# A gated attention and mixture-of-experts block: the running maximum spread by transfers and masked on GpSimd instead of by matmuls

## The chip, the cores and the metric

The kernel runs on one core of a Trainium2 chip. The metric is device time in microseconds (us). Before the change it is 1078.76 us, the median of three runs (1076.42 to 1082.22).

## The reference

For 16 batch elements of 256 tokens and 512 features, x goes through a gated mLSTM attention (8 heads of 64) against ctx, and then through a mixture of 16 experts (2 per token) with a shared expert. Cut to what matters here:

```
ig, fg = [q,k,v] @ gate weights + bias          # q = layernorm(x), k = v = ctx; per head and token
cs     = cumsum(log_sigmoid(fg))                # along the tokens
log_D  = cs[s] - cs[t] + ig[t], for t <= s, else -inf
D      = exp(log_D - max_t(log_D))
C      = (q k^T / 8) * D
h      = C v / (max(|sum C|, exp(-max)) + 1e-6)
x      = x + tanh(g0) * layernorm(h) * ln_scale
x      = x + tanh(g1) * (top-2 of 16 experts(layernorm(x)) + shared(layernorm(x)))
```

With key[t] = ig[t] - cs[t], the exponent is key[t] - M[s], where M[s] is the running maximum of key up to s. The kernel holds scores with t on the partitions and s along the row. So it needs M, one row per head, on all 128 partitions, and a very large value where s < t, so that the exponential gives zero there.

## The kernel before

One program has three stages: a loop over the 16 batch elements (attention, router, shared expert), the routed experts over 79 tiles of 128 rows, and a last stage that does the shared expert for four late batches (9, 11, 13, 15) and combines. Each engine has its own list of instructions, written out by hand in a function `step`, and waits on semaphores (`event`).

A step t of the loop holds work of several batches at once: A = t attends, F = t+1 is prepared (`turn_ctx`, `turn_x`, gates, `rows`, `columns`), N = t+2 gets its input statistics, G = t-1 is normalized after the attention, routed and put through the first half of its shared expert, H = t-2 has the second half of its shared expert, is ranked, and its rows are scattered to its experts in DRAM. For the late batches the shared expert is left out of the loop, so that steps 10, 12 and 14 lack `shared(G, 0)` and `shared(G, 1)`, and steps 11, 13 and 15 lack the shared work of H.

M is made on VectorE by a scan over 8 rows (`rows`, L1464). It is then split into three bf16 parts: ACT rounds the first (`max_hi`, L769), VectorE makes the other two (`rows_end`, L1472, L1475, L1477). PE spreads each head's M over the partitions (`spread`): for each head one product with a selecting matrix for 256 columns and one for 128 (L1091), and after each a product that adds the mask (L1093), into one of two PSUM banks, `MB`. ACT reads that bank in `head` (L782, L784) and writes the decay exp(key - M); VectorE multiplies it with the scores (`head`, L1492); PE multiplies with the values (`pv`, L1103 to L1106). PE's spreads stand in four blocks of two heads in a step: before `shared(H, 2)`, before `pv(A, 0)`, before `scores_pair(A, 2)`, and before `gates_sum(F)`. A pair of heads has one pair of score banks, `QK`, so `scores_pair(A, q)` waits until VectorE is done with pair q-1.

On GpSimd a step has the two small powers for G, the four indirect scatters of H, the copy of F's values (`values`, L567) and the power for N, in that order. SP's list holds the loads of ctx and x (`load_next`), 4 MB of zeros and a pad of 256 KB for the experts' rows (L457, L459), and the store of the shared weights in two parts, `kept_w` (L462). `load_next(b)` waits for the copy of batch b-2's values.

After the loop VectorE makes the tables of tiles, then the low part of expert 0's weights (L1841), then adds the last batch's shared sums and weighs. GpSimd issues the last eight scatters and then splits expert 1's weights. ACT issues the loads of the first four tiles of rows (16 transfers, L412) and then copies the tiles that VectorE has turned (L919); SP loads the later tiles. PE begins with `gate_up` (L1289).

## Time and profile before

| what | us |
|---|---|
| median of three runs | 1078.76 (1076.42 to 1082.22) |
| the profiled execution | 1078.9 |
| its span in the profile | 1077.3 |
| PE busy | 960.1 (89%) |
| VectorE (DVE) busy | 813.8 (76%) |
| ScalarE (ACT) busy | 424.7 (39%) |
| GpSimd (POOL) busy | 423.3 (39%) |
| attention loop, start to the last step's end | about 0 to 580 |
| routed experts | about 616 to 970 |
| late shared expert and combination | about 970 to 1077 |

Busy time is the time in which an engine has an instruction under way; matmuls overlap each other and their ends are modelled. The span is what the profile covers of the execution. An engine's share is a mean over stages with different limits, so that the rows are read by stage.

### The profile page before, as it was taken

Reading aid. Unit: us, or ns where it says so; the run is one execution under the profiler, and the core shown is the slowest. Engines: PE = TensorE matmul, PEld = TensorE weight load, DVE = VectorE, ACT = ScalarE, POOL = GpSimd, SP = SyncE. Lnnn points to the kernel's source line nnn. Section 1 sums busy time; section 2 is a strip of 40 time slices with the busy share of each in tenths; the row PEclk is TensorE's granted clock in tenths of the full one; section 3 lists DMA queues with packets and bytes.
Section 4 is the critical chain, followed back from the end, with each engine's and each line's share of the span. In section 5 each row is a group of like instructions: output and inputs, shape, how many; then the busy total and the mean of one; then the engine's idle time right before and its main releaser. Section 6 shows DMA issues by size and latency. Waiting matters only on the chain.

```text
span 1077.3 us, 21069 instructions
## 1 busy us (share of the span) xinstructions
PE 960.1 (89%) x6143; PEld 804.9 (75%) x6143; DVE 813.8 (76%) x1995; ACT 424.7 (39%) x957; POOL 423.3 (39%) x315
## 2 busy tenths in 40 slices
PE   3589999999999998989987199999999999999981
PEld 2479888988888886967777178888888888777761
DVE  2887889888988899888867666666666666655885
ACT  2654445444544455444522034444444444342110
POOL 5010220222022202222123907767767777104775
PEclk9989999999999998989969599999999999999996
DMA  8670211221122112111014455577667675924888
GB/s 256 223 287 2 80 40 40 79 79 40 40 79 79 39 42 79 60 59 41 11 42 159 159 169 179 179 211 212 180 183 228 177 206 155 335 77 149 261 284 263
DMA packets 92778, 147.26 MB, mean 137 GB/s; under 512 B 10720, under 2 KB 51168, under 8 KB 91776
## 3 DMA queue, kind: packets, MB, share of 16 engines
q0 software_dynamic: 17872, 65.02, 18.7%
q1 hardware_dynamic: 60592, 58.74, 17.3%
q10 hardware_dynamic: 14208, 22.16, 5.9%
q8 instruction: 57, 0.93, 0.4%
q14 instruction: 49, 0.40, 0.1%
HBM read 89.26 MB, written 56.62 MB: 135 GB/s over the span
## 4 chain that ended last, share of the span: by engine, by line
PE 69%; DVE 12%; issue 7%; DMA 4%; POOL 4%; ACT 1%; ACTq 1%; SPq 0%; DVEq 0%; POOLq 0%
PE bank L1289 19%; PE bank L1159 13%; PE bank L1308 9%; PE bank L1172 5%; PE bank L1082 4%; PE bank L1014 4%; POOL w_ring L698 3%; PE bank L1103 2%; PE bank L1106 2%; PE bank L1104 2%; PE bank L1356 2%; DMA x2n<-routed_x 2%; PE bank L1132 2%; PE bank L1299 2%; DMA base_out<-in_x_dram 2%
## 5 line engine op out<-in xcount | busy, mean ns | idle before, releaser
L1289 PE MATMUL bank<-w_ring,x2nT 128*128 x948 | 254.0, 406 | 19.9 <-DVE x2nT L1871 19.6
L1289 PEld LDWEIGHTS bank<-w_ring,x2nT 128*128 128x128 f32 x948 | 173.2, 190 | 57.7 <-issue 22.4
L1159 PE MATMUL bank<-x2nT,w_ring 128*128 128x256 f32 x1152 | 149.8, 286 | 0.0
L579 POOL DMA_INDIRECT routed_x<-x2n,slot_u x64 | 68.9, 1077 | 205.6 <-DVE slot_u L1632 190.6
L1159 PEld LDWEIGHTS bank<-x2nT,w_ring 128*128 128x128 f32 x1152 | 142.4, 190 | 0.3
L1308 PE MATMUL bank<-w_ring,sh_actT 128*128 x474 | 121.1, 391 | 3.5 <-DVE sh_actT L1860 3.5
L1860 DVE TENSOR_TENSOR sh_actT<-bank,sh_actT 128x256 fp32r<-128x256 f32 x79 | 33.5, 425 | 108.8 <-ACT sh_actT L929 108.8
L661 POOL TENSOR_TENSOR w_ring<-area,one 128x3072 fp32r<-128x3072 f32 x14 | 74.2, 5303 | 87.3 <-PE bank L1308 87.3
L1308 PEld LDWEIGHTS bank<-w_ring,sh_actT 128*128 128x128 f32 x474 | 88.8, 188 | 24.0 <-issue 4.6
L698 POOL DMA_INDIRECT w_ring<-routed_y,y_slot x64 | 67.8, 1060 | 77.6 <-DMA routed_y<-cs_in 52.6
L664 POOL TENSOR_TENSOR w_ring<-area,w_ring 128x3072 fp32r<-128x3072 f32 x14 | 95.8, 6845 | 2.5 <-POOL w_ring L661 2.5
L1866 DVE STREAM_TRANSPOSE bank<-x2n 128x512 f32<-128x512 f32 x79 | 86.6, 1096 | 3.6 <-DMA x2n<-routed_x 3.5
L934 ACT COPY cs_in<-bank 128x512 f32<-128x512 f32 x79 | 46.4, 588 | 84.2 <-PE bank L1308 77.3
L1172 PE MATMUL bank<-w_ring,sh_actT 128*128 128x512 f32 x288 | 72.5, 401 | 5.5 <-issue 5.5
L1492 DVE SCALAR_TENSOR_TENSOR area<-bank,area 128x384 f32<-128x384 f32 x128 | 65.8, 551 | 11.5 <-PE bank L1082 6.2
L586 POOL TENSOR_TENSOR x_rstd_all<-x_var,minus_half 128x2 f32<-128x2 f32 x16 | 12.8, 799 | 152.6 <-DVE x_var L1556 152.6
L923 ACT ACTIVATE ctxT<-bank 128x256 f32<-128x256 f32 x79 | 30.3, 384 | 102.7 <-PE bank L1289 102.7
L1082 PE MATMUL bank<-area,ctxT 64*128 64x256 f32 (+1 forms) x512 | 66.8, 377 | 0.0
L1172 PEld LDWEIGHTS bank<-w_ring,sh_actT 128*128 128x128 f32 x288 | 52.7, 190 | 17.9 <-issue 7.6
L782 ACT ACTIVATE area<-bank,key_log 128x256 f32<-128x256 f32 x128 | 61.0, 477 | 10.3 <-PE bank L1093 7.3
L1103 PE MATMUL bank<-area 128*128 128x65 f32 x256 | 51.3, 283 | 10.9 <-DVE area L1492 8.8
L1871 DVE TENSOR_TENSOR x2nT<-bank,x2nT 128x512 fp32r<-128x512 f32 x79 | 54.6, 691 | 7.9 <-ACT x2nT L919 3.0
(224 smaller groups left out, 1962.0 us busy)
## 6 DMA issues: line engine op xcount, KB each, us to landing
routed_y<-cs_in ACTq DMA_DIRECT2D x79, 256.0 KB, 2.9
x2n<-routed_x SPq DMA_DIRECT2D x300, 64.0 KB, 2.7
base_out<-in_x_dram SPq DMA_DIRECT2D x16, 512.0 KB, 5.1
cs_in<-in_ctx_dram SPq DMA_DIRECT2D x16, 512.0 KB, 4.1
area<-n_L_ffn_expert_gate_dram POOLq DMA_DIRECT2D x16, 512.0 KB, 5.3
area<-in_L_ffn_expert_up_dram POOLq DMA_DIRECT2D x16, 512.0 KB, 6.8
area<-n_L_ffn_expert_down_dram POOLq DMA_DIRECT2D x16, 512.0 KB, 8.4
out_dram<-base_out SPq DMA_DIRECT2D x32, 256.0 KB, 3.9
```

Of the source, the lines that this page charges most:

```text
L579: pool.indirect_dma_start(out=routed_x, in_=x2n[:, b.par, j, :], in_offset=None, out_offset=bass.IndirectOffsetOnAxis(ap=slot_u[:, b.par, ...
L661: g.tensor_tensor(w_ring[:, k, 0, :], stage[k], one[:, :].to_broadcast([P, EW]), ALU.mult).then_inc(expert_hi_in.sem, 1)
L664: g.tensor_tensor(w_ring[:, k, 1, :], stage[k], w_ring[:, k, 0, :], ALU.subtract).then_inc(expert_in.sem, 1)
L698: pool.indirect_dma_start(out=y_in[k][:, c, :], in_=routed_y, out_offset=None, in_offset=bass.IndirectOffsetOnAxis(ap=y_slot[:, at:at + 1] ...
L1082: last = mm(QK[k][:, at:at + n], ctxT[half, b.par, q, frm:frm + P], xnT[half, b.par, q, S - n:S], start=True, stop=True)
L1103: mm(HO[:, r:r + VW], cmat[:, k, 0:P], v_aug[:, b.par, 0, h, :], start=True, stop=True)
L1159: last = mm(gu_bank(b.n, m)[:, at:at + S], w[:, w_part, c, m * P:(m + 1) * P], x2nT[:, x_part, c, :], start=(c + p == 0), stop=(c == DC - ...
L1172: last = mm(down_bank(b.n, j)[:, :], sh_actT[:, x_part, m, j * P:(j + 1) * P], sh_down[:, w_part, m, :], start=(m + p == 0), stop=(m == SC ...
L1289: last = mm(bank[2 + t.par][:, :], xtT[:, x_part, t.par, c * P:(c + 1) * P], w_gu[:, bass.ds(slot, 1), w_part, c, :].rearrange("p a i -> p ...
L1308: last = mm(bank[5 + t.par][:, :], act_aT[:, x_part, t.par, c * P:(c + 1) * P], w_dn[:, bass.ds(slot, 1), w_part, c, :].rearrange("p a i - ...
L1492: v.scalar_tensor_tensor(cmat[:, k, :], QK[k][:, 0:TRI], QK_SCALE, decay[:, k, :], ALU.mult, ALU.mult).then_inc(c_made.sem, 1)
L1866: v.transpose(bank[t.par][:, :].rearrange("p (c g t) -> p g c t", c=DC, t=QP), xt[:, k, :].rearrange("p (g d c) -> p g c d", c=DC, d=QP)). ...
```

## The change

M goes through DRAM. SP stores the scan's 8 rows in a tensor `max_rows` (`max_store`) and loads two heads at a time, broadcast to all partitions, into one of two halves of `max_spread` (`max_load`): 256 columns of each head, and once more the last 128. GpSimd writes the mask into the first part with one select over 128x512 (`mask`). ACT's `head` reads `max_spread` in place of PSUM. A load for pair q waits until ACT is done with pair q-2.

PE's `spread`, ACT's `max_hi` and VectorE's last three operations of `rows_end` go, and so do the constants that they used. The two banks `MB` become a second pair of score banks, and `scores_pair(A, q)` waits for pair q-2. The step on GpSimd has a new order: h_stats(G), the masks of A's pairs 2 and 3, the values of F, x2_stats(G), stats(N), the scatters of H, the masks of F's pairs 0 and 1.

After the loop SP issues all row loads, ACT none. VectorE makes expert 0's low part after the shared sums and `weigh`. GpSimd waits for that low part before it rounds expert 1's weights, not after. The tables `row_tab` and `expert_tab` lie in the memory of `logit_row`.

```diff
+    max_rows = nc.dram_tensor("max_rows", (2, NH, S), F32).ap()
-        TP, SM, MB, QK, HO, FF = bank[0], bank[1], bank[2:4], bank[4:6], bank[6], bank[7]
+        TP, SM, QK, HO, FF = bank[0], bank[1], (bank[4:6], bank[2:4]), bank[6], bank[7]
+        max_spread = sb("max_spread", [P, 2, 2 * ST + 2, P])
...
+            def max_store(b):
+                sp.wait_ge(row_step.sem, row_step.upto(b.n, 4))
+                sp.dma_start(max_rows[b.par], max_row[:, :]).then_inc(max_out.sem, 16)
+            def max_load(b, q):
+                k, lap = q % 2, b.n * 2 + q // 2
+                sp.wait_ge(max_out.sem, max_out.upto(b.n))
+                sp.wait_ge(decay_made.sem, decay_made.upto(b.n, 2 * q - 2))
+                two = max_rows[b.par, 2 * q:2 * q + 2, :]
+                sp.dma_start(max_spread[:, k, 0:2 * ST, :].rearrange("p (h j) n -> p h (j n)", h=2),
+                             two.partition_broadcast(P)).then_inc(max_in[k].sem, 16)
+                sp.dma_start(max_spread[:, k, 2 * ST:, :], two[:, P:S].partition_broadcast(P)
+                             ).then_inc(max_in[k].sem, 16)
+            def max_front(b):
+                max_store(b)
+                max_load(b, 0)
+                max_load(b, 1)
+            def max_back(b):
+                max_load(b, 2)
+                max_load(b, 3)
             load_next(Item(0, 2))
+            max_front(Item(0, 0))
+            max_back(Item(0, 0))
             load_next(Item(0, 3))
...          (zeros and pad)
+            max_front(Item(0, 1))
...          (kept_w)
             for b in range(4, B):
...
+                max_back(Item(0, b - 3))
                 load_next(Item(0, b), more=b + 2 < B)
+                max_front(Item(0, b - 2))
+            for b in range(B - 3, B):
+                max_back(Item(0, b))
+                if b + 1 < B:
+                    max_front(Item(0, b + 1))
...
-            for n in range(XRING, TILES):
-                sp.wait_ge(xt_turned.sem, xt_turned.upto(n - XRING))
+            for n in range(TILES):
+                if n >= XRING:
+                    sp.wait_ge(xt_turned.sem, xt_turned.upto(n - XRING))
                 load_tile(n, n % XRING)
...
+            def mask(b, q):
+                k, lap = q % 2, b.n * 2 + q // 2
+                pool.wait_ge(max_in[k].sem, max_in[k].upto(lap))
+                own = max_spread[:, k, 0:2 * ST, :]
+                g.affine_select(out=own, in_=own, compare_op=ALU.is_ge, fill=MASK, base=0,
+                                pattern=[[0, 2 * ST], [1, P]], channel_multiplier=-1).then_inc(max_masked.sem, 1)
...          (GpSimd's step)
+                if attend:
+                    mask(A, 2)
+                    mask(A, 3)
+                if front:
+                    values(F)
                 if route:
                     x2_stats(G)
+                if ahead:
+                    stats(N)
                 if rest and route:
                     scatter(H)
                 if front:
-                    values(F)
-                if ahead:
-                    stats(N)
+                    mask(F, 0)
+                    mask(F, 1)
...          (ACT)
-                act.wait_ge(max_spread.sem, max_spread.upto(b.n, h + 1))
+                act.wait_ge(max_masked.sem, max_masked.upto(b.n * 4 + h // 2))
-                s.activation(decay[:, k, 0:S], MB[k][:, 0:S], ACT.Exp,
+                s.activation(decay[:, k, 0:S].rearrange("p (j n) -> p j n", j=ST),
+                             max_spread[:, h // 2 % 2, k * ST::2 * ST - k, :], ACT.Exp,
...          (PE)
-                pe.wait_ge(c_made.sem, c_made.upto(b.n, 2 * q))
+                pe.wait_ge(c_made.sem, c_made.upto(b.n, 2 * q - 2))
-            def spread(b, h):
...          (VectorE, after the loop)
+            shared_down(Item(0, LAST), 0)
+            shared_down(Item(0, LAST), 1)
+            weigh(Item(0, B - 1))
             dve.wait_ge(expert0_hi_in.sem, expert0_hi_in.upto(0))
             v.tensor_tensor(w_ring[:, 0, 1, :], stage[0], w_ring[:, 0, 0, :], ALU.subtract
                             ).then_inc(expert_in.sem, 1)
-            shared_down(Item(0, LAST), 0)
-            shared_down(Item(0, LAST), 1)
-            weigh(Item(0, B - 1))
```

## Rows read from the trace of the kernel before

**Rows 1.** Windows, one middle step: stretch, length, busy by engine, PEclk, DMA share, GB/s.

```profile
225.20:261.25 36.05, 35.32 (x295) 31.28 (x294) 32.04 (x95) 16.69 (x40) 7.62 (x8) 1.00 0.17 60
```

**Rows 2.** Timeline, PE: start, length, engine, line, operation; first of four spread blocks.

```profile
233.90 0.28 PE L1091 MATMUL bank<-max_parts,head_sel 96*128 96x256 bf16 x1
...
234.45 3.12 PE L1159 MATMUL bank<-x2nT,w_ring 128*128 128x256 f32 x24
```

**Rows 3.** Timeline, VectorE, the same step; in brackets the idle before and its releaser.

```profile
228.54 0.42 DVE L1637 SCALAR_TENSOR_TENSOR sh_act<-silu_t,bank 128x256 f32<-128x256 f32 x1 [0.45 <-ACT silu_t L798]
...
231.00 1.79 DVE L1646 SCALAR_TENSOR_TENSOR sh_actT<-sh_act,sh_actT 128x256 fp32r<-128x256 f32 x1
...
237.72 0.42 DVE L1646 SCALAR_TENSOR_TENSOR sh_actT<-sh_act,sh_actT 128x256 fp32r<-128x256 f32 x1
...
244.78 0.55 DVE L1442 TENSOR_SCALAR xn<-base_out,ln_mv,ln_rstd 128x512 f32<-128x512 f32 x1 [0.39 <-PE bank L1014]
```

**Rows 4.** Chain of waits, the same step: start, length, what.

```profile
249.86 0.47 DVE x2n L1564
```

**Rows 5.** Timeline, GpSimd, then ACT, the same step.

```profile
231.45 1.06 POOL L567 COPY area<-cs_in 128x1024 f32<-128x1024 f32 x1
...
239.50 0.39 ACT L784 ACTIVATE area<-bank,key_log 128x128 f32<-128x128 f32 x1
```

**Rows 6.** Groups by form: line, operation, shapes, count, busy us, mean ns, idle.

```profile
L504 POOL TENSOR_SCALAR_AFFINE_SELECT head_sel<-head_sel 128x1024 bf16<-128x1024 bf16 x3 | 3.3, 1094 | 0.4
```

**Rows 7.** DMA issues: what, queue, count, KB each, median us to landing.

```profile
routed_y<-cs_in ACTq DMA_DIRECT2D x79, 256.0 KB, 2.9
...
kept_w<-w_ring SPq DMA_DIRECT2D x2, 3072.0 KB, 19.5
...
x2n<-routed_x ACTq DMA_DIRECT2D x16, 64.0 KB, 1.9
...
routed_x<-base_out SPq DMA_DIRECT2D x1, 256.0 KB, 14.2
```

**Rows 8.** Timelines at the start: VectorE's scans, ACT's first decays, PE's gates.

```profile
28.83 0.68 DVE L1464 TENSOR_TENSOR_SCAN max_row<-key_max 8x256 f32<-8x256 f32 x1
...
52.78 0.68 DVE L1464 TENSOR_TENSOR_SCAN max_row<-key_max 8x256 f32<-8x256 f32 x1
...
32.62 0.47 ACT L782 ACTIVATE area<-bank,key_log 128x256 f32<-128x256 f32 x1 [0.93 <-PE bank L1093]
...
59.31 0.47 ACT L782 ACTIVATE area<-bank,key_log 128x256 f32<-128x256 f32 x1 [1.05 <-PE bank L1093]
...
69.88 0.64 PE L1055 MATMUL bank<-area,gate_wT 128*32 128x256 f32 x8
```

**Rows 9.** Timeline at the start, SP's issues.

```profile
39.19 0.37 SPq L426 DMA_DIRECT2D cs_in<-in_ctx_dram  x1
...
42.54 5.20 SPq L459 DMA_DIRECT2D routed_x<-base_out  x1
...
48.11 2.22 SPq L462 DMA_DIRECT2D kept_w<-w_ring  x2
```

**Rows 10.** Hand-over: timelines of VectorE, GpSimd, ACT, PE, and one chain piece (DMA).

```profile
596.86 3.34 DVE L1841 TENSOR_TENSOR w_ring<-area,w_ring 128x3072 fp32r<-128x3072 f32 x1
...
596.96 4.08 POOL L579 DMA_INDIRECT routed_x<-x2n,slot_u  x1 [0.30 <-issue]
...
601.34 2.70 DMA routed_x<-x2n,slot_u
...
605.04 9.27 ACTq L412 DMA_DIRECT2D x2n<-routed_x  x16
...
610.94 1.11 DVE L1866 STREAM_TRANSPOSE bank<-x2n 128x512 f32<-128x512 f32 x1 [1.36 <-DMA x2n<-routed_x]
...
616.00 4.63 PE L1289 MATMUL bank<-w_ring,x2nT 128*128 x10 [19.58 <-DVE x2nT L1871]
```

**Rows 11.** PE's timeline in step 11, and the window after it.

```profile
426.29 0.18 PE L1116 MATMUL bank<-chosen,before_b 128*128 128x16 bf16 x1 [1.43 <-DVE taken_mid L1597]
...
428.00:432.00 4.00, 4.00 (x20) 3.27 (x20) 3.24 (x12) 1.61 (x3) 0.00 (x0) 0.50 0.00 0
```

More of the change, by code:

```diff
@@ L231, in flamingo_kernel @@
         first_tab = sb("first_tab", [1, E], I32)
-        row_tab = sb("row_tab", [1, P], I32)
-        expert_tab = sb("expert_tab", [1, P], I32)
+        row_tab, expert_tab = (logit_row[0:1, k * P:(k + 1) * P].bitcast(I32) for k in range(2))
         xt = x2n[:, :, :, :].rearrange("p a j d -> p (a j) d")
@@ L262, in turn_bank @@
         def turn_bank(b, j):
[L263 removed]
+            return QK[0][1] if b == B - 1 and j else TP
         def router_bank(b):
[L266 removed]
+            return QK[1][1] if b == B - 1 else SM
         def down_bank(b, j):
@@ L271, in gu_bank @@
         def gu_bank(b, m):
-            return MB[0] if b == LAST and m == SC - 1 else GU[m]
+            return QK[1][0] if b == LAST and m == SC - 1 else GU[m]
         small_in = event("small_in", 16)
@@ L305, in flamingo_kernel @@
         key_made = event("key_made", 2)
-        row_step = event("row_step", 8)
-        max_hi_made = event("max_hi_made")
+        row_step = event("row_step", 5)
+        max_out = event("max_out", 16)
+        max_in = [event(f"max_in{k}", 32) for k in range(2)]
+        max_masked = event("max_masked")
         columns_turned = event("columns_turned")
@@ L906, in _ @@
             s.copy(w_ring[:, 0, 0, :], stage[0]).then_inc(expert0_hi_in.sem, 1)
-            act.wait_ge(tables_made.sem, tables_made.upto(0))
-            for par in range(2):
-                act.wait_ge(scattered[par].sem, scattered[par].upto(B // 2 - 1))
-            for n in range(XRING):
-                row = act.value_load(row_tab[0:1, n:n + 1], min_val=0, max_val=DUMP)
-                load_rows(act, row, n)
             def copy_x(t):
@@ L1081, in scores_pair @@
                         half = slice(DH * k, DH * (k + 1))
-                        last = mm(QK[k][:, at:at + n], ctxT[half, b.par, q, frm:frm + P],
+                        last = mm(QK[q % 2][k][:, at:at + n], ctxT[half, b.par, q, frm:frm + P],
                                   xnT[half, b.par, q, S - n:S], start=True, stop=True)
                 last.then_inc(qk_made.sem, 1)
-            def spread(b, h):
-                k = h % 2
-                pe.wait_ge(row_step.sem, row_step.upto(b.n))
-                pe.wait_ge(decay_made.sem, decay_made.upto(b.n, h - 1))
-                for at, n in ((0, S), (S, P)):
-                    mm(MB[k][:, at:at + n], head_sel[0:3 * FG, h, :], max_parts[0:3 * FG, b.par, S - n:S],
-                       start=True, stop=False)
-                    last = mm(MB[k][:, at:at + P], identb[:, :], mask_b[:, :], start=False, stop=True)
-                last.then_inc(max_spread.sem, 1)
             def pv(b, h):
@@ L1186, in step @@
                     scores_pair(A, 0)
-                    spread(A, 0)
-                    spread(A, 1)
                 if rest:
@@ L1193, in step @@
                 if attend:
-                    spread(A, 2)
-                    spread(A, 3)
                     pv(A, 0)
@@ L1205, in step @@
                 if attend:
-                    spread(A, 4)
-                    spread(A, 5)
                     scores_pair(A, 2)
@@ L1215, in step @@
                     gates_pe(F)
-                if attend:
-                    spread(A, 6)
-                    spread(A, 7)
                 if front:
@@ L1670, in count_rows @@
                 dve.wait_ge(counts_made.sem, counts_made.upto(0))
-                then(v.tensor_copy(count[:, :], QK[0][:, 0:E]))
+                then(v.tensor_copy(count[:, :], QK[0][0][:, 0:E]))
             def piece(k):
```

45 lines of the change are left out of this document (8 added, 37 removed).

## The prediction

> **What bounds the kernel now.** I read the page first, then the windows by stage, then one middle step in the chain of waits and on each engine, then the start and the hand-over to the experts. Over a step of the attention loop PE is busy 35.32 of 36.05 us and VectorE 32.04 [rows 1]. That looks like a loop bound by PE, and the spreading that goes is PE work: four blocks a step, of 0.55 us (233.90 to 234.45 [rows 2]) to 0.68, about 2.5 us a step and 39 us in 16. The chain decides whether that is a gain. Up to 244.7 PE has no gap, but VectorE is hardly behind: its one idle stretch there is the 0.39 us before its second `norm_front` [rows 3]. From there the chain runs through VectorE until x2n is normalized at 250.33 and PE can turn it [rows 4]. All four blocks lie ahead of that. So PE can be ready there 2.5 us sooner, and the step still ends with VectorE's list: what comes back is VectorE's idle 0.39 us. The rest of the step is PE's, and no spread is in it.
>
> **The change part by part.**
>
> *Spreads off PE, double score banks.* Gain at least 0 (if VectorE has no slack) and at most 2.5 us a step (if PE alone bound it). I take 0.39, from VectorE's idle row [rows 3].
>
> *Three small VectorE operations and ACT's rounding of the maximum go.* They work on the scan's 8 rows, and the scan takes 0.68 us [rows 8], so at most 2.0 us a step. They stand just before a VectorE wait of 0.45 us for ACT's tanh, which waits for PE [rows 3]: in that stretch PE covers VectorE. I take 0; if PE no longer covered it, the gain would be up to 2.0.
>
> *Masks on GpSimd.* Four selects a step over 128x512. The trace has selects of 1024 elements in 1.09 us [rows 6]; half of that and a fixed part is 0.64 us, my estimate (bounds 0.55 and 1.09). GpSimd has room. The price is on VectorE: while GpSimd copied the values (1.06 us from 231.45 [rows 5]), a VectorE operation on two SBUF tensors that began at 231.00 took 1.79 us, where its like takes 0.42 [rows 3]. Today that stands under PE's cover. Now two masks and the values copy come between the fourth head's decay (done at 239.89 [rows 5]) and x2_stats, in VectorE's own stretch: the transfer for pair 3 starts at 239.9, lands about 243.2, mask to 243.9, copy to 244.9, and `norm_front` could have begun at 244.4. The mask of pair 2 comes at about 240, among `center`'s operations. Cost: 0 if they fall beside operations on PSUM, up to 2 x 0.64 + 1.06 = 2.3 us if each holds VectorE for its length; I take 0.5, the overlap of copy and `norm_front`. Net with the gain: +0.1 us a step, over 13 steps +1.4; bounds -5 (no collision) and +25.
>
> The Trainium skill (SBUF — State Buffer, SBUF: two separate sides) calls the pair of ports that VectorE and GpSimd share an exclusive lock, which the loser waits out for the whole instruction. The 1.79 us row agrees; by that rule alone, if each mask met such an operation, 13 steps would cost about +20 us instead of +1.4.
>
> *Transfers, start of the loop.* Before, the scan of batch 0 ends at 29.51 and head 0 decays at 32.62 [rows 8]. Now a store of 8 KB, two broadcast loads (384 KB) and a mask lie between. No such transfer is in the trace: nearest are 64 KB in 1.9 and 256 KB in 2.9 us [rows 7]. The scan comes 0.67 sooner, since the values copy no longer stretches the operation before it: 28.84 + 1.9 + 0.5 (second issue) + 2.9 + 0.64 + 0.1 = 34.9, +2.3 us. In a middle step the same transfers run while PE works, and they are back about when GpSimd is through with its scatters.
>
> *SP's queue.* All loads and stores of the maximum go into SP's queue, and it serves in order: 256 KB behind the 4 MB of zeros landed after 14.2 us, where the 256 KB of a tile take 2.9 [rows 7]. (a) `load_next(3)` now waits for the values copy behind mask 3, about 44.9 instead of 39.19, so zeros and pad end at 42.54 [rows 9] + 14.2 + 5.7 = 62.4 instead of 56.7. Batch 1's maximum is scanned at 53.46 [rows 8] + 2.3 and a little mask contention = 56.5; its store lands not at 58.5 but at 62.6. With loads and mask the first decay of batch 1 is at 66.4 instead of 59.31 [rows 8], +7.1. (b) kept_w, 6.3 MB, issued at 48.11 [rows 9], now follows at 64.5. It took until 67.6 (19.5 us [rows 7], the first 8 behind the zeros): somewhat over 11 us by itself, and I take 14.5, until 80, since part of it had moved beside the zeros. The loads for pairs 2 and 3 of batch 1 are queued behind it: they land at 81.3, mask to 82.0, heads 4 and 5, then ACT's copy of xn for batch 2, and PE's `gates_pe` starts at 84.0 instead of 69.88 [rows 8]. That chain of gates is what is late next: +14.1 us in all. Bounds: +2.3 if the queue let small transfers pass, +17 with a slower kept_w.
>
> *Scatters ahead of the next masks.* Four issues as before, for slots made at the same time, until 231.45, where the values copy starts today [rows 5]. The next batch's first two masks follow to 232.8, before the spreads that they replace have ended (234.45 [rows 2]). Nothing; late masks would cost what they are late. Values, and with them the loads of ctx and x, move some 20 us earlier: nothing. The 24.6 MB of new traffic falls into a stage with 60 GB/s [rows 1].
>
> *Hand-over.* Two edits, both on the path. VectorE's subtraction for expert 0 (596.86, 3.34 us) ran while GpSimd issued its seventh scatter, which took 4.08 us instead of 0.96 [rows 10]. It now follows two sums and `weigh`, 2.0 us later: the last scatter starts at 598.2 instead of 601.34 and lands (2.70) at 600.9: -3.1. Then ACT issued 16 row loads in 9.27 us from 605.04 and only after them copied tile 0, though tile 1 had been there at 610.94 [rows 10]. With SP issuing, tile 1 lands at 607.8; VectorE turns it (1.1), takes tile 0's rest (0.7), and PE starts at 609.9 instead of 616.00 [rows 10]: -6.1 in all. Bounds -3 (the scatter stays blocked) and -8. GpSimd's new wait for expert 0's low part ends at about 602.3, when its first split began anyway; behind it stand the splits for expert 1, needed only after PE's first tiles.
>
> The Trainium skill (SBUF — State Buffer, SBUF: two separate sides) says that VectorE keeps GpSimd from writing descriptors while it runs a 2-port mode. The subtraction reads two tensors and is none, yet the row shows 4.08 us; the row decides. By the sentence's wording alone this part would be about -3.
>
> **Sum.** Against the profiled execution, 1078.9 us (span 1077.3 and 1.6 around it; the median of the runs is 1078.76): 1078.9 + 14.1 (start) + 1.4 (steps) - 6.1 (hand-over) = 1088.3, said as 1088.
>
> **Rivals.**
> - *The queue lets the small transfers through, and the masks miss VectorE.* 1078.9 + 2.3 - 5 - 6.1 = 1070. For it: the store is 8 KB. Against: rows 7. Faster. 0.16.
> - *PE was the bound.* Half or more of the 39 us comes: 1078.9 + 14.1 - 6.1 and less 20 to 39 = 1048 to 1067. For it: PE's 98%. Against: rows 3 and 4. Faster. 0.04.
> - *Half of the start's cost is hidden*, for kept_w's pieces let the loads in between: 1078.9 + 7 - 6.1 = 1080. Within the bound. 0.20.
> - *PE's clock falls.* PE would now wait some 2 us between 244 and 250 in each step. At 426.29, after a wait of 1.43 us for VectorE, and from 428 to 432 the granted clock stood at 0.50 [rows 11], the lower of the two levels, 1.2 GHz. If that comes in each of 9 dense steps, the 5 us of PE's work after 250 take 10 with 0.6 of slack, and a step is 2 to 4 us longer: 1088 + 18 to 36, about 1112. [...] Slower. 0.14.
> - *The forecast*, 1088, with 1080 to 1097 for itself: 0.46.
>
> About 0.5% (5.4 us) is what a measurement of this kernel can tell from no change. Faster: 0.16 + 0.04, less the first rival's upper tail = 0.18. Slower: 0.46 + 0.14, less the forecast's lower tail = 0.57. Same: the rest, 0.25. The range reaches from the first rival to near the clock's: 1070 to 1107.
>
> **What would show it.** Right: first decay of batch 0 near 35, `gates_pe` of the second step near 84 with PE idle some 8 us before; DMA busy with kept_w from 64 to 80; middle steps of 35.6 to 36.7 us with PE waiting before `turn_x(F,1)` and before it turns x2n; first expert matmul 6 us nearer to the end of the loop. Wrong: middle steps of 34 us (PE was the bound) or of 38 with a clock below 1 (the rival); loads of batch 1 landing within 4 us although kept_w is under way.

## The result and the profile after

The changed kernel takes 1104.24 us (median of 4 runs, 1103.40 to 1106.00) against 1077.61 us (4 runs of the kernel before beside it, 1076.42 to 1082.22): ratio 1.0231, 95% interval 1.0194 to 1.0268. The forecast was 1088, in a range of 1070 to 1107. Slower was right; +26.6 us is nearly three times the +9.4 of the forecast. Medians count every execution and ratios the fast ones alone; the two differ in the kernel early_loads below, whose median is 1083.51 us without one slow execution of 2796.09.

The profiled execution took 1106.0 us, its span is 1104.4, 27.1 longer than before. Its busy times:

```profile
PE 950.2 (86%) x5631; PEld 787.8 (71%) x5631; DVE 784.4 (71%) x1947; ACT 427.6 (39%) x941; POOL 453.6 (41%) x370
```

PE has 9.9 us less to do and VectorE 29.4, and yet the time grew, by waits and by products that take longer. The scans of the maximum (L1464 before, L1467 after) are good marks, for each batch has one. Between them and the points after the loop the 27.1 us lie like this:

| stretch | before | after | difference | forecast |
|---|---|---|---|---|
| start to scan of batch 2 | 79.92 | 104.35 | +24.43 | +14.1 |
| scan 2 to scan 11 (nine steps) | 323.98 | 320.65 | -3.33 | +1.4, scan 2 to 15 |
| scan 11 to scan 12 | 28.81 | 34.64 | +5.83 | in the +1.4 |
| scan 12 to scan 15 | 99.87 | 100.50 | +0.63 | in the +1.4 |
| scan 15 to the turn of the last x2n | 48.42 | 50.08 | +1.66 | 0 |
| from there to the first expert matmul | 35.00 | 31.30 | -3.70 | -6.1 |
| experts and last stage | 461.3 | 462.9 | +1.6 | 0 |

The windows of the changed kernel (columns as in [rows 1]): scan 0 to scan 1, scan 1 to scan 2, two middle steps, scan 11 to scan 12, and the hand-over.

```profile
28.81:60.85 32.04, 21.84 (x104) 16.61 (x104) 19.98 (x41) 18.09 (x33) 4.50 (x6) 1.00 0.57 172
60.85:104.35 43.50, 26.67 (x131) 21.24 (x132) 21.92 (x59) 12.42 (x28) 5.53 (x8) 0.80 0.64 242
210.53:245.87 35.34, 33.21 (x262) 29.03 (x262) 29.68 (x92) 16.83 (x39) 9.91 (x12) 1.00 0.32 105
317.62:353.71 36.09, 33.26 (x262) 29.05 (x262) 30.40 (x92) 16.95 (x39) 10.12 (x12) 1.00 0.37 103
425.00:459.64 34.64, 27.73 (x156) 21.81 (x155) 25.90 (x78) 14.07 (x31) 9.59 (x12) 0.66 0.30 92
610.22:641.52 31.30, 12.03 (x55) 9.53 (x56) 19.45 (x68) 6.06 (x9) 20.14 (x16) 0.66 0.54 192
```

In a middle step PE is busy 33.2 us where [rows 1] have 35.32, and the step is as long as before or 0.7 shorter. In the first two windows PE is busy 22 of 32 and 27 of 44 us.

The chain of waits at the start of the changed kernel (start, length, what), which answers to [rows 8]:

```profile
61.55 4.67 DMA max_rows<-max_row
66.62 5.02 DMA max_spread<-max_rows
74.43 15.22 DMA max_spread<-max_rows
92.52 1.98 PE bank L1076 x16
```

The store of batch 1's 8 KB takes 4.67 us, the loads for its first pair 5.02, those for pair 2 15.22, and the gates start at 92.52 (69.88 before, 84.0 in the forecast). ACT's first decay of batch 0 starts at 36.59, forecast 34.9.

The step of batch 11, on GpSimd, then PE (timelines):

```profile
431.88 0.96 POOL L608 DMA_INDIRECT routed_x<-x2n,slot_u  x1 [0.30 <-issue]
432.85 1.22 POOL L597 TENSOR_SCALAR_AFFINE_SELECT max_spread<-max_spread 128x512 f32<-128x512 f32 x2
```
```profile
435.08 0.44 PE L1114 MATMUL bank<-area 128*128 128x65 f32 x2 [3.12 <-DVE area L1487]
```

PE waits 3.12 us in front of the first `pv` of batch 11, and from about 436 until the scan of batch 12 (459.64) its granted clock is 0.50, the lower of its two levels (1.2 GHz). In the kernel before the clock is 0.50 in this period too, but only from 409 to 413 and from 427 to 433 [rows 11]. One of the windows:

```profile
445.00:449.00 4.00, 4.00 (x26) 3.24 (x28) 3.11 (x15) 0.58 (x1) 0.69 (x1) 0.50 0.42 123
```

A row of `pv` is a pair of products that overlap. At the upper level it lasts 0.39 us and the next row starts 0.22 us after it; at the lower level these are 0.63 and 0.43. So the rows tell the level also where the granted clock does not.

The first `pv` of batch 11 comes 10.08 us after that batch's scan, where it came 9.67 us after it before. So 0.4 of the 5.83 us lie ahead of it, and 5.4 behind it, in the stretch at the lower level: 24.56 us from there to the scan of batch 12, where the kernel before took 19.14.

The hand-over, GpSimd, chain, and PE:

```profile
627.74 0.96 POOL L608 DMA_INDIRECT routed_x<-x2n,slot_u  x1 [0.30 <-issue]
```
```profile
629.00 3.48 DMA routed_x<-x2n,slot_u
```
```profile
641.52 6.25 PE L1291 MATMUL bank<-w_ring,x2nT 128*128 x15 [14.33 <-DVE x2nT L1866]
```

### The profile page after: what moved, and what is told of

It reads as the page before. It is cut to its first block, busy times and chain, and to the rows that moved or that the text cites. A ratio compares the mean times of both kernels' runs of the same rounds, so it can differ in the third digit from the quotient of the medians.

```text
span 1104.4 us, 20171 instructions
## 1 busy us (share of the span) xinstructions
PE 950.2 (86%) x5631; PEld 787.8 (71%) x5631; DVE 784.4 (71%) x1947; ACT 427.6 (39%) x941; POOL 453.6 (41%) x370
## 4 chain that ended last, share of the span: by engine, by line
PE 57%; DVE 19%; issue 10%; DMA 5%; POOL 5%; ACT 2%; SPq 1%; DVEq 0%; POOLq 0%; ACTq 0%
PE bank L1291 19%; PE bank L1310 9%; PE bank L1170 7%; PE bank L1183 5%; POOL w_ring L733 3%; DVE area L1487 2%; PE bank L1035 2%; PE bank L1358 2%; DMA x2n<-routed_x 2%; DVE base_out L1536 2%; DMA max_spread<-max_rows 2%; PE bank L1103 2%; PE bank L1114 2%; PE bank L1143 2%; PE bank L1117 2%
## 5 line engine op out<-in xcount | busy, mean ns | idle before, releaser
L1291 PE MATMUL bank<-w_ring,x2nT 128*128 x948 | 254.4, 407 | 14.8 <-DVE x2nT L1866 14.3
L608 POOL DMA_INDIRECT routed_x<-x2n,slot_u x64 | 63.2, 988 | 116.8 <-DVE slot_u L1627 101.9
L597 POOL TENSOR_SCALAR_AFFINE_SELECT max_spread<-max_spread 128x512 f32<-128x512 f32 x64 | 42.5, 669 | 152.1 <-DMA max_spread<-max_rows 151.9
L1487 DVE SCALAR_TENSOR_TENSOR area<-bank,area 128x384 f32<-128x384 f32 x128 | 66.0, 552 | 35.3 <-ACT area L815 15.5
L1114 PE MATMUL bank<-area 128*128 128x65 f32 x256 | 55.5, 302 | 29.5 <-DVE area L1487 26.0
L812 ACT ACTIVATE area<-max_spread,key_log 128x256 f32<-128x256 f32 x128 | 64.2, 502 | 31.9 <-POOL max_spread L597 31.4
L1103 PE MATMUL bank<-area,ctxT 64*128 64x256 f32 (+1 forms) x512 | 73.2, 408 | 0.0
L1114 PEld LDWEIGHTS bank<-area 128*128 128x128 f32 x256 | 44.7, 218 | 34.9 <-DVE area L1487 30.4
```

The costliest lines, as they stand in the source:

```text
L812: s.activation(decay[:, k, 0:S].rearrange("p (j n) -> p j n", j=ST), max_spread[:, h // 2 % 2, k * ST::2 * ST - k, :], ACT.Exp, bias=key_l ...
L1103: last = mm(QK[q % 2][k][:, at:at + n], ctxT[half, b.par, q, frm:frm + P], xnT[half, b.par, q, S - n:S], start=True, stop=True)
L1114: mm(HO[:, r:r + VW], cmat[:, k, 0:P], v_aug[:, b.par, 0, h, :], start=True, stop=True)
L1291: last = mm(bank[2 + t.par][:, :], xtT[:, x_part, t.par, c * P:(c + 1) * P], w_gu[:, bass.ds(slot, 1), w_part, c, :].rearrange("p a i -> p ...
L1487: v.scalar_tensor_tensor(cmat[:, k, :], QK[h // 2 % 2][k][:, 0:TRI], QK_SCALE, decay[:, k, :], ALU.mult, ALU.mult).then_inc(c_made.sem, 1)
```

## The experiments

Each run was compared with runs of the kernel before on its own chip. "Scan 2" is the start of batch 2's scan, "11 to 12" the period between those two scans, from the run's profile. Kernels whose start is that of the kernel before have scan 2 at 79.92, 82.64 and 81.12, so a difference of 3 us there says nothing by itself.

| kernel | median us | ratio to before (95%) | scan 2 | 11 to 12 |
|---|---|---|---|---|
| changed kernel | 1104.24 | 1.0231 (1.0194 to 1.0268) | 104.35 | 34.64 |
| kept_later | 1096.21 | 1.0140 (1.0110 to 1.0170) | 97.91 | 34.58 |
| start_order | 1094.42 | 1.0103 (1.0064 to 1.0143) | 94.23 | 34.46 |
| act_queue | 1102.34 | 1.0195 (1.0173 to 1.0217) | 104.38 | 34.47 |
| warm | 1095.63 | 1.0141 (1.0100 to 1.0181) | 94.47 | 34.24 |
| warm_short | 1089.65 | 1.0082 (1.0056 to 1.0108) | 88.00 | 34.57 |
| warm_all | 1087.53 | 1.0060 (1.0039 to 1.0081) | 89.28 | 31.74 |
| early_loads | 1083.98 | 1.0027 (1.0000 to 1.0054) | 83.86 | 31.87 |
| early_warm | 1083.08 | 1.0033 (1.0008 to 1.0059) | 84.00 | 31.48 |
| early_warm2 | 1081.54 | 1.0009 (0.9988 to 1.0030) | 80.57 | 34.23 |
| early_masks | 1078.52 | 1.0006 (0.9977 to 1.0034) | 80.22 | 32.71 |
| masks_first | 1105.49 | 1.0234 (1.0201 to 1.0268) | 103.97 | 34.37 |
| no_mask | 1096.45 | 1.0144 (1.0113 to 1.0176) | 102.56 | 30.92 |
| single_bank | 1105.35 | 1.0212 (1.0166 to 1.0258) | 102.78 | 34.10 |
| handover_alone | 1074.32 | 0.9946 (0.9922 to 0.9970) | 82.64 | 28.27 |
| handover_filled | 1076.42 | 0.9953 (0.9928 to 0.9978) | 81.12 | 28.13 |

**The large transfers at the start.** kept_later:

```diff
             max_front(Item(0, 1))
-            for part in range(2):
-                sp.dma_start(kept_w[part], ...)
             for b in range(4, B):
                 max_back(Item(0, b - 3))
+                if b == 4:
+                    (kept_w, both parts)
                 load_next(Item(0, b), more=b + 2 < B)
```

> The changed kernel with one move: SP stores the 6.3 MB of kept_w behind the loads for pairs 2 and 3 of batch 1 instead of ahead of them. Theory (the order of SP's queue makes most of the 24.4 us that the start lost): those loads land within 5 us instead of 15.2, gates_pe of the second step starts near 82 instead of 92.5, and the time falls by about 9 us, to 1095. Rival (the start is long because every round trip is slow and PE runs at its lower level): the loads come sooner, but PE, at the lower level, is what is late next, and only 3 to 4 us come back, about 1101.

Measured 1096.21, the theory's number, but the gates start at 86.08, not near 82, and scan 2 comes 6.4 us sooner, not 9. With kept_w issued directly behind them, the loads for pair 2 are through, and masked, 4.8 us after their issue (SP's issues, then GpSimd's mask):

```profile
73.80 0.32 SPq L460 DMA_DIRECT2D max_spread<-max_rows  x1
...
76.64 0.94 SPq L490 DMA_DIRECT2D kept_w<-w_ring  x2
```
```profile
78.60 0.64 POOL L598 TENSOR_SCALAR_AFFINE_SELECT max_spread<-max_spread 128x512 f32<-128x512 f32 x1 [4.38 <-DMA max_spread<-max_rows]
```

start_order makes one more move:

```diff
             max_back(Item(0, 0))
-            load_next(Item(0, 3))
             (zeros, pad)
+            load_next(Item(0, 3))
             max_front(Item(0, 1))
```

> The changed kernel with two moves in SP's list: kept_w behind the loads for pairs 2 and 3 of batch 1, and the zeros and the pad ahead of the third load of ctx, so that they are issued near 43 instead of 50 and are through before the maximum of batch 1 is stored. Theory (queue order): the store of batch 1's maximum takes about 1.3 us instead of 4.7 and its loads 4 instead of 5, some 4.5 us besides those of kept_w alone: 13 to 14 us less than the changed kernel, about 1091. Rival (slow round trips, PE at the lower level): 4 us less, about 1100, and hardly more than with kept_w moved alone.

Scan 2 comes 10.1 us sooner than in the changed kernel, 6.4 by kept_w and 3.7 by the zeros. The store of batch 1's maximum is issued at 61.39 and its first load at 62.72, 1.33 us later, where it was 4.67. The 3.7 us are hardly more than the scatter of scan 2, and the intervals of the two ratios overlap, but the store's 3.3 us go the same way. The median, 1094.42, lies between theory and rival: 14.3 of the 24.4 us are still there.

act_queue asks whether it is SP's queue at all:

```diff
                 if attend:
                     head(A, 1)
+                if attend and A.n == 1:
+                    (ACT issues kept_w, both parts)
```

> The changed kernel, with kept_w issued by ACT at the same place in time (behind the first two decays of batch 1, near 73) instead of by SP, so that its 6.3 MB are still ahead of the loads for pairs 2 and 3 of batch 1 but in another queue. Theory (it is SP's queue that serves in order): the loads land in 4 to 8 us while kept_w is under way, and the time is that of kept_w moved behind them, about 1096. Rival (the 16 DMA engines are full, whatever the queue): the loads land after about 13 us as before, and the time stays above 1102.

The rival was right: the delay does not need SP's queue. ACT's issues, SP's, and GpSimd's next mask:

```profile
70.70 0.36 ACTq L851 DMA_DIRECT2D kept_w<-w_ring  x1
```
```profile
72.07 0.32 SPq L460 DMA_DIRECT2D max_spread<-max_rows  x1
```
```profile
89.83 0.63 POOL L594 TENSOR_SCALAR_AFFINE_SELECT max_spread<-max_spread 128x512 f32<-128x512 f32 x1 [17.31 <-DMA max_spread<-max_rows]
```

From another queue, kept_w, issued 1.4 us ahead of them, holds the loads up until 89.8, 17.8 us after their issue. What counts here is which transfer was issued first, not on which of the two queues. The Trainium skill (DMA: Bandwidth & Descriptors, Queues, rings and completion order) has the 16 engines take turns between queues a packet at a time; the trace agrees. From 76 to 86 us ACT's queue (q10) moved 175 packets of kept_w, some 22 KB each, and SP's queue (q1) 166 small ones (packets, MB, share of the 16 engines):

```profile
q10 hardware_dynamic: 175, 3.91, 92.4%
q1 hardware_dynamic: 166, 0.27, 7.2%
```

So the loads do get turns while kept_w is under way, about one small packet for each large one, and that makes them as late as standing behind it. In the changed kernel, where both are in SP's queue, they do stand behind it: in the same 10 us only 31 of 202 packets are under 8 KB, against 182 of 342 here.

**PE's level at the start.** warm adds products that nobody reads, in the bank `FF`, which is free then:

```diff
+            def fill(b, n):
+                for _ in range(n):
+                    mm(FF[:, 0:S], ctxT[:, b.par, 0, 0:P], xnT[:, b.par, 0, :], start=True, stop=True)
                 if attend:
                     scores_pair(A, 0)
+                if attend and A.n < 2:
+                    fill(A, FILL[A.n])
```

> The kernel with both moves in SP's list, and besides PE gets products whose result nobody reads (24 of 128x256 before the first pv of batch 0, 12 before that of batch 1), so that it does not stand idle while the maximum is stored, loaded and masked. Theory (half of what the start still loses is PE at its lower level: its products there take 0.43 us a pair, where the kernel before has 0.22): with the wait filled PE comes to the upper level as in the kernel before, the pairs take 0.22, the scan of batch 2 comes 4 to 6 us sooner (near 89 instead of 94.2), and the time is about 1089. Rival (the round trips alone make it): PE's products are shorter but the chain waits for the loads and masks, and the time stays within 2 us of 1094.

By its time the rival was right: an idle product took 0.49 us, so that the fill outlasted the wait, and the first `pv` of batch 0 came at 43.2 instead of 37.9, and that of batch 1 at 76.1 instead of 70.05. But from there to scan 2 it took 18.4 us instead of 24.2. The row behind that is one line of `pv`, start_order first, then warm:

```profile
70.54 0.63 PE L1116 MATMUL bank<-area 128*128 128x65 f32 x2
```
```profile
76.27 0.39 PE L1116 MATMUL bank<-area 128*128 128x65 f32 x2
```

warm_short puts 10 such products before the columns of batch 0 and sizes the others to the waits (11 and 5).

> The kernel with both moves in SP's list and idle products on PE as before, now sized to the waits they fill: 10 of 128x256 in the 5.66 us before the columns of batch 0, 11 in the 5.41 us before its first pv, 5 before that of batch 1 (such a product took 0.49 us at the lower level). Theory (PE at its lower level costs some 6 us in each of the first two steps: with PE at the upper level the stretch from the first pv of batch 1 to the scan of batch 2 took 18.4 us instead of 24.2): PE runs at the upper level in one or both steps without a later first pv, the scan of batch 2 comes at 84 to 89 instead of 94.2, and the time is 1084 to 1090. Rival (fills of this length do not raise the level, or do not hold it over the next wait): scan of batch 2 at 93 to 96, time 1092 to 1096.

Theory: scan 2 at 88.00, 6.2 us sooner than in start_order. The median is 4.8 us lower, though the intervals of the two ratios overlap.

**The round trip.** early_loads, on start_order, reads a large constant that is in DRAM from the start:

```diff
-                sp.wait_ge(max_out.sem, max_out.upto(b.n))
+                sp.wait_ge(max_out.sem, 32)
             def max_front(b):
-                max_store(b)
```

> The kernel with both moves in SP's list, with the round trip cut out: the maximum is not stored; the loads read rows of a large constant that stand in DRAM from the start, so they wait only until their half of the buffer is free. Loads, masks, traffic and every engine's order stay (the decay is zero, so attention's result is left out). Theory (the round trip from scan to masked rows is what the start and the step of batch 11 wait for): the first decay of batch 0 comes at 32 or before, the scan of batch 2 near 82 (80 in the kernel before), the period from the scan of batch 11 to that of batch 12 is 29 us again, and the time is 1074 to 1078. Rival (masks on GpSimd, their collisions with VectorE and PE's lower level keep the start long): the scan of batch 2 later than 88 and the time above 1085.

Scan 2 at 83.86, 10.4 us sooner, and 1083.98: between the two. The rows of `pv` still last 0.63 us through the first step, though PE never stands idle for 1 us in it. early_warm adds the idle products.

> All three causes of the longer start taken away at once: SP's list with both moves, loads of a large constant that need not wait for the scan (attention's result is left out, as in the kernel with early loads), and idle products on PE (10 of 128x256 before the columns of batch 0, 2 and 3 before the first pv of batches 0 and 1). Theory (queue order, round trip and PE's level are all of the 24.4 us): the scan of batch 2 comes at 79 to 82, where the kernel before has 79.9, against 83.9 without the idle products, and the time is 1078 to 1082. Rival (a fourth cause, masks or traffic, remains): the scan of batch 2 stays at 83 or later and the time at 1084 or above.

The theory failed as put: scan 1 was where it is before (53.30), but PE fell again in the second step and scan 2 stayed at 84.00. early_warm2 fills that step too.

> The kernel with both moves, early loads and idle products, with more of these: 6 of 128x256 before the second turn of x in the first two steps, and 12 before the seventh pv of batch 0, where PE waited 1.2 to 4.75 us and fell to its lower level (attention's result is left out, as before). Theory (queue order, round trip and level are all of what the start lost): PE's pairs take 0.22 us in most of the second step, the scan of batch 2 comes at 79 to 81.5, and the time is 1078 to 1081. Rival (masks or traffic are a fourth cause): although PE is at its upper level there, the scan of batch 2 stays at 83 or later.

Now PE keeps its upper level through most of the second step, and scan 2 stands at 80.57 (PE, then VectorE); the time, 1081.54, is half a microsecond above the theory's.

```profile
69.13 0.33 PE L1119 MATMUL bank<-area 128*128 128x65 f32 x2
```
```profile
80.57 0.68 DVE L1484 TENSOR_TENSOR_SCAN max_row<-key_max 8x256 f32<-8x256 f32 x1
```

That is the kernel before within its own scatter: the place of the large transfers, the round trip and PE's level are all of the 24.4 us. The level's part with the trips gone, 3.3 us, is no larger than that scatter; with the trips in place it was 6.2.

**The step of batch 11.** masks_first:

```diff
+                if front:
+                    mask(F, 0)
+                    mask(F, 1)
                 if rest and route:
                     scatter(H)
-                if front:
-                    mask(F, 0)
-                    mask(F, 1)
```

> The changed kernel with GpSimd's masks for pairs 0 and 1 of the next batch ahead of the four scatters instead of behind them. Theory (the order on GpSimd makes the step of batch 11 5.8 us longer): pair 0's mask there is done about 2 us sooner, PE's wait of 3.12 us ahead of pv falls below 1.4, its granted clock stays at 1.00 as far as in the kernel before, and 5 to 6 us come back, about 1099. Rival (the round trip through DRAM is what is late): the loads themselves land hardly before the scatters are through, pair 0's mask comes at most 1 us sooner, the clock still falls, and less than 2 us come back, 1102 to 1106.

The rival was right. The mask's wait is now the transfer's, and it starts 7.01 us after the scan of batch 11 (425.62), only 0.8 sooner than in the changed kernel:

```profile
432.63 0.64 POOL L597 TENSOR_SCALAR_AFFINE_SELECT max_spread<-max_spread 128x512 f32<-128x512 f32 x1 [11.03 <-DMA max_spread<-max_rows]
```

warm_all has the fills of early_warm2 on real transfers, and 11 products before the first `pv` of batches 11, 13 and 15.

> The kernel with both moves in SP's list, all of the changed kernel's transfers and masks, and idle products on PE at all these places of the first two steps and, 11 of them, before the first pv of batches 11, 13 and 15, where PE waits for the mask of pair 0. Theory (the level that PE falls to after these waits costs more than the waits): the scan of batch 2 comes at 84 to 88 (88.0 with the first fills), the period from the scan of batch 11 to that of batch 12 falls from 34.6 to about 31 us, and the time is 1079 to 1085. Rival (in step 11 the wait itself is the cost, and the level falls at the next wait anyway): that period stays above 33.5 us, and the time is 1086 to 1090.

The period is 31.74, 2.9 us shorter, and the rows of `pv` after the fill last 0.39 us:

```profile
422.22 0.33 PE L1115 MATMUL bank<-area 128*128 128x65 f32 x2
422.39 0.39 PE L1116 MATMUL bank<-area 128*128 128x65 f32 x2
```

The level is worth more than the 2.9, since the fill itself makes `pv` late: it comes 11.62 us after the scan (410.60), 1.5 later than in the changed kernel. From there to the scan of batch 12 it takes 20.12 us, against 24.56 in the changed kernel and 19.14 in the kernel before, so 4.4 of those 5.4 us are the level. Scan 2, 89.28, missed the theory's 84 to 88, and the time, 1087.53, is the rival's.

Two kernels above show the same without a fill. early_loads and early_warm2 have the same instructions in this step; over the period the mean granted clock is 0.72 in the one and 0.57 in the other, and the period is 31.87 and 34.23 us. Without the round trip, too, the period is the longer, the longer PE is at the lower level.

early_masks takes away round trip and scatters at once (early_warm2 with the masks first).

> The kernel with both moves, early loads and idle products in the first two steps, and besides GpSimd's masks for pairs 0 and 1 of the next batch ahead of the four scatters (attention's result is left out, as before). With either taken away alone, PE still waited 2.2 to 3.1 us for pair 0 in the step of batch 11: the mask came 7.9 us after the start of the scan with early loads (behind the scatters) and 7.0 us with the masks first (behind the round trip). Theory (two waits that end together, each hiding the other): with both away pair 0 is masked before the scan, PE's wait there is under 1 us, the period from the scan of batch 11 to that of batch 12 is 28 to 29.5 us as in the kernel before, and the time is about 1073 to 1078. Rival (PE is let down there by something else, its lower level or VectorE's list): that period stays above 31 us and the time at 1080 or above.

My theory of two waits that hide each other fell in its main number. Pair 0 is masked at 398.14, 4 us before the scan of batch 11 (402.26), and PE still waits:

```profile
411.34 0.44 PE L1119 MATMUL bank<-area 128*128 128x65 f32 x2 [2.10 <-DVE area L1504]
```
```profile
410.73 1.02 DVE L1504 SCALAR_TENSOR_TENSOR area<-bank,area 128x384 f32<-128x384 f32 x2
```

ACT's decays end at 410.05, but VectorE's list has the statistics of the batch before (408.96 to 410.78) ahead of the first product. So `pv` comes 9.1 us after the scan, and 10.1 in the changed kernel: the late mask is worth 1.0 us. The kernel before has `pv` 9.67 us after its scan, between the two, with no wait at all, since PE makes spreads until then:

```profile
410.65 0.40 PE L1091 MATMUL bank<-max_parts,head_sel 96*128 96x256 bf16 x1
...
413.57 0.44 PE L1103 MATMUL bank<-area 128*128 128x65 f32 x2
```

**Masks against VectorE.** no_mask reads a constant and cuts the mask to 128x8 elements:

```diff
-                own = max_spread[:, k, 0:2 * ST, :]
+                own = max_spread[:, k, 0:2 * ST, 0:2]
```

> The changed kernel with the mask cut from 128x512 elements to 128x8 (the loads read rows of a large constant, so that the decay is zero; the store of the maximum, its wait and all transfers stay; attention's result is left out). Theory (the masks of pairs 2 and 3 stretch VectorE's operations on two SBUF tensors, and which steps they hit makes the difference between middle steps of 35.35 and 36.0 us): all middle steps take 35.35 or less, 3 us less in nine of them, and the start some 2 us less for the shorter masks: about 1099. Rival (the later loads or the values copy make the longer steps): middle steps still alternate, and no more than 2 us come back.

Theory, as to the middle steps: seven of the nine take 35.32 to 35.36 us (the first 34.60, the last 35.70), and the mean from scan 2 to scan 11 is 35.30 us, against 35.63 with masks. Two stand here. The time falls further than the theory's 1099, to 1096.45, since the step of batch 11 is 3.7 us shorter too (30.92); there `pv` comes 9.68 us after the scan, and the granted clock is back at 1.00 from 440 to 450 (0.50 in the changed kernel).

```profile
313.87:349.23 35.36, 33.24 (x262) 29.08 (x262) 29.45 (x92) 16.84 (x39) 8.09 (x12) 1.00 0.32 105
349.23:384.55 35.32, 33.23 (x262) 29.01 (x262) 29.46 (x92) 16.84 (x39) 8.03 (x12) 1.00 0.34 106
```

The collision itself, in the 36.09 us step of the changed kernel, GpSimd and VectorE:

```profile
335.70 0.63 POOL L597 TENSOR_SCALAR_AFFINE_SELECT max_spread<-max_spread 128x512 f32<-128x512 f32 x1 [3.82 <-DMA max_spread<-max_rows]
338.70 0.63 POOL L597 TENSOR_SCALAR_AFFINE_SELECT max_spread<-max_spread 128x512 f32<-128x512 f32 x1 [2.37 <-DMA max_spread<-max_rows]
339.28 1.23 POOL L589 COPY area<-cs_in 128x1024 f32<-128x1024 f32 x1
```
```profile
335.79 1.75 DVE L1536 SCALAR_TENSOR_TENSOR base_out<-area,h_rstd,base_out 128x512 f32<-128x512 f32 x2
...
338.68 0.93 DVE L1444 TENSOR_SCALAR xn<-base_out,ln_mv,ln_rstd 128x512 f32<-128x512 f32 x1
```

In the 35.34 us step the same two take 1.40 and 0.54: together 0.74 of the 0.75 us. There the masks, at 228.16 and 232.18, begin beside operations that read PSUM (L1487, L1635). Where the loads land decides it.

**The second pair of score banks.** single_bank:

```diff
-                pe.wait_ge(c_made.sem, c_made.upto(b.n, 2 * q - 2))
+                pe.wait_ge(c_made.sem, c_made.upto(b.n, 2 * q))
```

> The changed kernel with the scores of pair q waiting for pair q-1 again instead of q-2, so that the second pair of score banks is not used ahead. Theory (in a middle step PE waits for VectorE, not for a bank): middle steps stay at 35.35 to 36.1 us and the time within 2 us of the changed kernel's. Rival (the second pair of banks is what gave the middle steps their 0.4 us): they go back to 36.0 or above in every step, and the time rises by 3 to 6 us.

Theory: 1105.35, and the middle steps have a mean of 35.67 us, against 35.63. The banks gave nothing that can be measured.

**The hand-over.** handover_alone is the kernel before with the three edits after the loop (the last hunks of the diff).

> The kernel before with only the three edits after the loop (VectorE's low part of expert 0 behind the last sums and weigh, SP issues all row loads, GpSimd waits for that low part first). Theory: both gains of the forecast are real and do not depend on the rest of the change. The seventh scatter takes 0.96 us instead of 4.08, the first expert matmul comes 9 us after the last scatter has landed instead of 12: from the turn of the last x2n to the first expert matmul 29 us instead of 35.0, and 6 us less in all, about 1072. Rival: the same stretch took 31.3 us in the changed kernel, so something besides (PE at the lower clock in the last router, a slower landing of the scatter) belongs to the edits, and the gain is 3.7 us, about 1075.

5.8 us less by the ratio (3.2 to 8.4): it beats both kernels. The seventh scatter takes 0.96 us, the last lands, and PE begins 9.0 us later (GpSimd, chain, PE):

```profile
597.24 0.96 POOL L580 DMA_INDIRECT routed_x<-x2n,slot_u  x1 [0.30 <-issue]
```
```profile
598.51 2.70 DMA routed_x<-x2n,slot_u
```
```profile
610.24 6.57 PE L1282 MATMUL bank<-w_ring,x2nT 128*128 x15 [13.55 <-DVE x2nT L1864]
```

From the turn of the last x2n (579.80) to that matmul it is 30.4 us, between the theory's 29 and the rival's 31.3: here too the twelve products of the shared sum ahead of the router take 4.65 us, where the kernel before has 3.17.

handover_filled adds 46 idle products of 128x128 in that wait.

> The kernel before with the three edits after the loop, and 46 idle products of 128x128 on PE behind the turn of the tables, in its 13.55 us wait for the first tile of rows. There the first 15 expert products took 6.57 us at a granted clock of 0.50, and later nine took 2.35. Theory (the level after an idle stretch is a cost of its own): the first 15 take about 4 us, and the time falls by 2 to 3 us below that of the three edits alone. Rival (the first tiles wait for their rows anyway, so a faster start is lost in the next wait): within 1 us of it.

The median, 1076.42, shows no gain, as the rival has it, but the intervals of the two ratios are wider than the 2 to 3 us in question. In the trace the gain is there and is not lost at the later tiles. The first 15 products take 3.76 us instead of 6.57, and the same later products, counted from the first, start 2.4 us sooner (34.77 us after it without the fill, 32.35 with it):

```profile
645.01 2.35 PE L1282 MATMUL bank<-w_ring,x2nT 128*128 x9
```
```profile
646.69 2.35 PE L1284 MATMUL bank<-w_ring,x2nT 128*128 x9
```

Whether the time falls is not settled.

## Why the prediction was right or wrong

**What bounds the loop: right.** PE lost 2.1 us of work in each middle step; the step fell from 36.00 to 35.63 in the mean of nine. The two terms were a gain of 0.39 and a collision of 0.5. Measured are 0.70 without masks (36.00 to 35.30) and 0.33 for them. The 0.39 was not VectorE's one idle stretch: it also stood idle for 0.45 us at 228.54 [rows 3], 0.54 at 229.95 and 0.65 at 233.44; whether those make up the rest is not shown. The mask takes 0.63, estimated 0.64. The rule of the Trainium skill on the shared ports (SBUF — State Buffer, SBUF: two separate sides), reckoned in the forecast at 20 us, doesn't show in that size: 0.33 a step is 4 us in 13, since the masks often meet an operation on PSUM and, where they don't, stretch VectorE's two operations by 0.74 us together.

**The start: the step that failed.** "28.84 + 1.9 + 0.5 (second issue) + 2.9 + 0.64 + 0.1 = 34.9, +2.3 us" priced one round trip of batch 0, and all that followed was charged to the queue. The queue's part was sized well, 11.8 of the 14.1 against 10.1 measured, though the order of SP's queue, the reason given, is only half of it: in that queue the loads do come behind kept_w, but kept_w in ACT's queue makes them as late. The other part was put at 2.3 us and is 14.3. Batch 0 alone was nearly right: its first decay comes at 36.59, and 0.65 of the 1.7 us are a scan that did not come sooner (it ends at 29.49, not 28.84). What failed is all that this one trip left out. First, every pair of batches 0 and 1 makes a trip on the chain, not the first alone; loads have a median of 3.7 us (256 KB) and 4.6 (the 128 KB behind them), where I took 3.4 for both. Taking the trips away gave 10.4 us. Secondly, PE's level: the spreads were what PE did in its waits. Without them the rows of `pv` start 0.43 us apart from 38 to 83 us, where in the kernel before they do so only from 54 to 57 and are 0.22 apart otherwise; filling the waits gave 6.2 us with the trips in place and 3.3 with the trips gone.

**"PE's clock falls" was a rival in the wrong place.** It was priced for the nine dense steps. There it never came: behind the first 3 us of the first of them the granted clock is 1.00 in all, and the longest wait of the step from 210.53 is 0.93 us. It came at the start, where PE waits 5.18, 2.78, 6.33 and 7.31 us, and in the step of batch 11, behind a wait of 3.12.

**"Nothing" for scatters ahead of masks.** The order is worth nothing, as said (masks_first, same time). But I looked only at a middle step, where the spreads' end at 234.45 [rows 2] left room. In the step of batch 11, which lacks H's shared work, nothing stands beside the masks: 5.83 us. Most of it is PE's level: 0.4 us lie ahead of the first `pv`, 5.4 behind it, and with the level held (warm_all) 4.4 of those 5.4 come back. Of the wait of 3.12 us ahead of it, 1.0 is the late mask and the rest VectorE's list, which the spreads had covered.

**The hand-over: both terms right, the sum short.** From first to last scatter 8.99 us instead of 12.11, -3.12 (forecast -3.1); from the landing to the first matmul 9.04 instead of 11.96, -2.92 (forecast -3.0). But the first scatter came 1.56 us later after the turn, since twelve products of the shared sum ahead of the router took 4.72 us instead of 3.17, and the last landing took 3.48 instead of 2.70. The slower products are no work of the transfers, for handover_alone has them too. Alone the edits bring -5.8 in time, -4.6 in this stretch.

So of the 17.7 us that the sum missed, 10.3 lie at the start, 3.4 in the loop behind it, 2.4 at the hand-over and 1.6 later. Not settled is what the last two rows of the loop (+0.63, +1.66) and the +1.6 consist of; they are of the size by which executions differ.

## What to carry to other kernels

Work that is taken off an engine is worth what the chain gives back, and it may have been filling a wait: when PE loses its filler, look at each place where it will now stand idle, and price what follows at the lower level of its clock, from rows at that level. A round trip through DRAM that hides in the steady state is bare in the first steps and in every step with less work, so price it there, for each pair. The 6.3 MB store held up the small loads issued after it from either of two queues, and not when it was issued behind them: look for that order first.

## What was not expected of the hardware

- The row of the granted clock can miss the lower level. From 38 to 83 us the changed kernel's windows say 1.00, while the rows of `pv` start 0.43 us apart, as at 0.50 elsewhere. In the page of no_mask, with the same start, the row does show it:

```profile
PEclk9556999999999997995978689999999999999996
```

  The Trainium skill (TensorE: Matmul & The Clock Gate, Part 1) warns that clock events in a trace are not reliable; durations decide.
- A transfer of 6.3 MB on ACT's queue delayed loads of 384 KB on SP's queue to 17.8 us from issue to mask; issued 0.5 us after the last of them, on SP's own queue, it did not (4.8 us). From the two queues the engines did take turns, about one small packet for each of 22 KB.
- A mask of 0.63 us on GpSimd stretched a VectorE operation by 0.35 to 0.39 us, less than its own length.
